# Issuing the small TensorE matmuls of the linear-attention stage one at a time between large ones

## The reference

```python
q = (x @ Wq.T).reshape(bsz, seq_len, H, HD).transpose(0, 2, 1, 3)
k = (x @ Wk.T).reshape(bsz, seq_len, KVH, HD).transpose(0, 2, 1, 3)
v = (x @ Wv.T).reshape(bsz, seq_len, KVH, HD).transpose(0, 2, 1, 3)
q = q * cos + _rotate_half(q) * sin
k = k * cos + _rotate_half(k) * sin
qf = jax.nn.elu(q) + 1.0
kf = jax.nn.elu(k) + 1.0
def step(carry, inp):
    state, z = carry
    q_s, k_s, v_s = inp
    state = state + k_s[..., :, None] * v_s[..., None, :]
    z = z + k_s
    num = jnp.einsum('bhe,bhed->bhd', q_s, state)
    den = jnp.einsum('bhe,bhe->bh', q_s, z)[..., None] + EPS
    return ((state, z), num / den)
```

## Time and profile before

| | |
|---|---|
| three runs | 2307.86, 2310.42, 2312.11 us (median 2310.42) |
| profiled execution | 2310.1 us from its first to its last instruction; its own whole time is listed nowhere else, and is taken as this span |
| first stage, fill (0 to 115 us) | TensorE waits for weights and inputs in part |
| first stage, steady (about 115 to 890 us) | 7 tiles of about 111 us |
| first stage, last tile and start of the second | about 890 to 962 us |
| rest | output projection, then the feed-forward, to 2310.1 us |
| busy over the span | TensorE 98%, weight loads 79%, VectorE 79%, ScalarE 55%, GpSimd 49% |

### The profile page before, as it was taken

One profiled execution on the slowest core, in us unless ns is written; L12 is line 12 of the kernel. 1 busy time (PEld: TensorE's weight loads), 2 busy tenths in 40 slices (PEclk: granted clock), 3 DMA queues, 4 the chain that ended last, 5 costly groups with the idle time before them and its releaser, 6 DMA issues.

```text
span 2310.1 us, 32819 instructions
## 1 busy us (share of the span) xinstructions
PE 2254.4 (98%) x10209; PEld 1823.0 (79%) x10209; DVE 1825.1 (79%) x2452; ACT 1273.1 (55%) x2285; POOL 1129.0 (49%) x1002
## 2 busy tenths in 40 slices
PE   7999999999999999999999989999999999999998
PEld 5778787787878786787777768888888888888887
DVE  7877777778686868787887896787888788878877
ACT  6666666666676767233334455454545554455443
POOL 4667676767676767455544733321242133303321
PEclk9999999999999999999999999999999999999999
DMA  4110101111120215777767541323233323222323
GB/s 153 37 65 37 68 34 66 47 58 62 39 73 28 73 60 192 255 246 254 245 229 261 187 140 62 123 78 113 79 101 92 118 81 98 92 82 83 98 67 101
DMA packets 132701, 252.75 MB, mean 109 GB/s; under 512 B 44576, under 2 KB 45344, under 8 KB 122880
## 3 DMA queue, kind: packets, MB, share of 16 engines
q1 hardware_dynamic: 132608, 251.60, 32.5%
HBM read 188.11 MB, written 63.44 MB: 109 GB/s over the span
## 4 chain that ended last, share of the span: by engine, by line
PE 71%; issue 11%; POOL 9%; DVE 5%; ACT 2%; DMA 1%; SPq 0%; POOLq 0%; ACTq 0%; DVEq 0%
PE pj L548 17%; PE pj L629 11%; PE pnum L629 6%; PE pj L643 5%; PE psc L629 5%; PE pj L558 4%; PE pst L629 4%; PE psc L643 4%; PE pnum L643 3%; PE psc L579 3%; PE pnum L597 3%; PE pnum L600 3%; PE pst L643 2%; POOL fa L1338 2%; PE pst L586 1%
## 5 line engine op out<-in xcount | busy, mean ns | idle before, releaser
L1368 POOL TENSOR_TENSOR wcs<-wcr 128x256 f32<-128x256 f32 x64 | 67.7, 1058 | 515.3 <-DVE wcl L1107 504.3
L1401 POOL TENSOR_TENSOR tb<-tb,sinb 128x512 f32<-128x512 f32 x160 | 224.0, 1400 | 91.7 <-ACT tb L928 90.9
L548 PE MATMUL pj<-xah,wqh 128*128 128x512 f32 x512 | 204.3, 399 | 4.3 <-DVE Kf L1243 3.0
L1404 POOL TENSOR_TENSOR Ql<-tb,Qh 128x512 fp32r<-128x512 f32 x128 | 169.7, 1328 | 70.2 <-ACT Qh L937 70.1
L478 PE MATMUL pj<-woh,oh 128*128 128x512 f32 x512 | 202.9, 396 | 0.0
L548 PE MATMUL pj<-xal,wqh 128*128 128x512 f32 x512 | 200.5, 392 | 0.0
L548 PE MATMUL pj<-xah,wql 128*128 128x512 f32 x512 | 200.5, 392 | 0.0
L478 PE MATMUL pj<-woh,ol 128*128 128x512 f32 x512 | 200.4, 391 | 0.0
L478 PE MATMUL pj<-wol,oh 128*128 128x512 f32 x512 | 200.3, 391 | 0.0
L1231 DVE TENSOR_TENSOR pj<-pj,cosb 128x512 f32<-128x512 f32 x160 | 111.1, 694 | 69.7 <-ACT tb L928 69.6
L629 PE MATMUL pj<-xch,wch 128*128 128x512 f32 x384 | 150.9, 393 | 7.9 <-DVE xcl L1113 4.7
(11 more groups left out here) (258 smaller groups left out, 7070.8 us busy)
## 6 DMA issues: line engine op xcount, KB each, us to landing
num_scratch<-no SPq DMA_DIRECT2D x128, 256.0 KB, 2.4
nt<-num_scratch SPq DMA_DIRECT2D x32, 1024.0 KB, 5.5
rb<-rden_scratch SPq DMA_DIRECT2D x32, 1024.0 KB, 6.3
wdr<-wd_scratch SPq DMA_DIRECT2D x128, 256.0 KB, 3.3
wcr<-in_wg SPq DMA_DIRECT2D x64, 256.0 KB, 2.8
wcr<-in_wu SPq DMA_DIRECT2D x64, 256.0 KB, 3.1
xst<-in_xT SPq DMA_DIRECT2D x34, 256.0 KB, 3.8
xr<-in_x SPq DMA_DIRECT2D x32, 256.0 KB, 5.6
```

The source lines that it names most:

```text
L548: last = nc.tensor.matmul(bank[:, :], w[:, b, :], x[:, b, :], start=(k == 0), stop=(k == 11))
L1401: nc.gpsimd.tensor_tensor(tb[c][:, :], tb[c][:, :], sinb[:, :], ALU.mult).then_inc(sin_done, 1)
L1404: nc.gpsimd.tensor_tensor(Ql[g % 2][:, c, :], (tb[c] if c else Kf)[:, :], f32(Qh[g % 2][:, c, :]), ALU.subtract).then_inc(lo_done, 1)
```

## The change

The 3 matmuls of a Z and the 4 transposes of a T are no longer issued where their event stands. The event only appends them to a list. The J, V, C and U events issue one from the head of the list after each of their large matmuls but the last (U's third matmul of the first half included); D issues none. The waits of a Z or a T are made directly ahead of its first small matmul, which is now inside another event. What is left in the list at the end of a tile's events is issued there. Each small matmul keeps its operands, its place among the small ones and its semaphore; the other engines' programs are as before.

```diff
+            def key_transpose(m, where, g, d, q):
+                if q == 0:
+                    bank_released(m, ("T", g, 0, d), where)
+                    pe.wait_ge(f_done, upto(m, d, NR, g * (G + 1)))
+                    if where == "start":
+                        pe.wait_ge(c_in, 16)
+                last = nc.tensor.transpose(pj[job_bank("T", g, 0)][:, q * CH:(q + 1) * CH], Kf[:, q * CH:(q + 1) * CH],
+                                           identb[:, :])
+                if q == NCH - 1:
+                    last.then_inc(t_done, 1)
+
+            def state_update(m, g, c, d, k):
+                u = g * NCH + c
+                hd = slice(g * HD, (g + 1) * HD)
+                if k == 0:
+                    pe.wait_ge(t_lo, upto(m, d, KV, g))
+                    pe.wait_ge(v_lo, upto(m, d, NCH, c))
+                    pe.wait_ge(s_lo, upto(m, d, NU, u))
+                a, b = ((Kth, Vh), (Kth, Vl), (Ktl, Vh))[k]
+                last = nc.tensor.matmul(pst[:, hd], a[:, c, :], b[:, c, hd], start=False, stop=(k == 2),
+                                        skip_group_check=True)
+                if k == 2:
+                    last.then_inc(state_done, 1)
...
+                short = []
+
+                def one_short():
+
+                    if short:
+                        kind, g, c, d, k = short.pop(0)
+                        if kind == "T":
+                            key_transpose(m, where, g, d, k)
+                        else:
+                            state_update(m, g, c, d, k)
+
                 for kind, g, c, d in events:
-                    if kind in "JVTD":
+                    if kind in "TZ":
+                        short += [(kind, g, c, d, k) for k in range(NCH if kind == "T" else 3)]
+                        continue
+                    if kind in "JVD":
...
                                 k += 1
+                                if k < 12:
+                                    one_short()
...
-                    elif kind == "T":
-                        pe.wait_ge(f_done, upto(m, d, NR, g * (G + 1)))
-                        if where == "start":
-                            pe.wait_ge(c_in, 16)
-                        for q in range(NCH):
-                            last = nc.tensor.transpose(bank[:, q * CH:(q + 1) * CH], Kf[:, q * CH:(q + 1) * CH], identb[:, :])
-                        last.then_inc(t_done, 1)
...
                             last = nc.tensor.matmul(out, a[:, 0, tok], b[:, 1:, tok], start=(k == 0), stop=(k == 2))
+                            if k < 2:
+                                one_short()
...
                             nc.tensor.matmul(num, a[:, c, hd], b[:, :, :], start=(k == 0), stop=False)
+                            one_short()
...
+                            if k < 2:
+                                one_short()
                         last.then_inc(unit_done, 1)
...
+                while short:
+                    one_short()
```

## The result

The changed kernel is slower: median 2331.2 us (2330.9 to 2333.0, 4 runs) against 2309.7 us of the kernel before in the same session (4 runs); ratio 1.009, 95% interval 1.0077 to 1.0103. The profiled execution is 2329.2 us long from first to last instruction, 19.1 us more than before. The forecast had the sign right and half of the size: 2320, range 2308 to 2328, and the measured time lies above that range.

The account below looks back on a forecast made before the run. TensorE was taken to set the pace of the first stage's seven steady tiles. The terms 3.9 + 2.4 - 0.3 + 0.7 + 3.0 = +9.7 us on the 2310.1 us span gave 2319.8, forecast as 2320, range 2308 to 2328.

Parts of the forecast that it names:

- The price of a small matmul: On TensorE a single small matmul costs 0.112 us as in a row, since weight loads run only one matmul ahead.
- The rival with loads further ahead: TensorE fetches weights further ahead, so small matmuls cost only their streaming time: -23 us, 2287 us; chance 0.10.
- The dearer exits: On TensorE, returning from small to large matmuls costs slightly extra, paid after each single one: +3.9 us over 8 tiles.
- Z22: Z22 moves behind U22's wait for `Al`, which had hidden it: +0.34 us in each of seven turns, +2.4 us.
- T3, C30 and J02: T3's transposes move behind C30's wait for `Ql`, -0.3 us; K3 comes late and J02 waits, +0.7 us.
- -0.3 us at C30: In three turns, two transposes behind C30's wait for `Ql` add 0.23 us each time, while 0.34 is absorbed.
- the slack of 0.7 us: Spare time, 0.70 us, before J02 starts at 583.99 and needs its bank; if it holds, late K3 costs J02 0.
- +0.7: J02 waits about 0.1 us per turn for its bank because K3 is late: +0.7 us.
- T2 ends about 1.1 us later: Later ends of T2, T0 and T1 cost nothing, as the next uses are 4 us or more behind.
- The last tile: A late fourth transpose delays K3 by 2.9 us, then VectorE's division and A30, which C32 awaits: +3.0 us.
- The rivals: Weights loaded further ahead, 2287 us (0.10); shifts mostly absorbed, about 2313 (0.25); keys late in every turn, 2328 (0.12).

Follow-up runs that it names:

- late rows: Changed kernel with each Z and T issued in a row again, at the place of its last single small matmul; 2331.3 us.
- singly in the loop only: Changed kernel with Z and T in rows in the unrolled tile before the loop and in the last tile, single only in the loop; 2322.5 us.

## Why the prediction was half right

- **The price of a small matmul.** Right: 0.114 us singly, 0.112 in a row, the large one behind it 0.45 us long, and the load one matmul ahead. The rival with loads further ahead is out by the changed kernel's own trace. The dearer exits, 3.9 us in the sum for eight tiles, were not far off: 2 to 3 us in seven turns, to which 3.4 of the 3.9 belong.
- **Z22.** Right in kind: the wait grew from 0.6 to 1.0 us in each of seven turns. But U22 itself starts 0.13 us earlier against D2, so only 0.23 us per turn stay, 1.6 us in all and not 2.4. For this move alone the times can't tell it from zero.
- **T3, C30 and J02.** The sum had -0.3 us at C30, taking its wait for `Ql` to occur in three turns only. The stretch around C30 costs +1.8. K3 does start over a microsecond late on ScalarE (a wait of 1.42 us in the turn at 477 us), but no wait of TensorE at J02 appears; the slack of 0.7 us held, so +0.7 was 0.
- **"T2 ends about 1.1 us later ... the next uses (Z20, J12, Z10) are 4 us or more behind, so I cost these at nothing."** This is the step that failed. I looked for who reads the result of the transposes and not for who waits to overwrite their input. VectorE's E30 writes `Kf` and waits for T2's end, and J32 waits for E30 with 0.08 us in hand. Seven times 0.80 us is 5.6 us, the largest single term of the loss; with T2 alone in a row 4.0 of them go.
- **The fill.** The prediction had no term for it. T1's lateness holds K1, the weight parts queue behind K1, and J21 waits 2.6 instead of 1.2 us and then runs at the lower clock: 3.8 us, of which the clock's 1.6 are in part luck.
- **The last tile.** Right in chain: C32 stands 2.7 us further behind C30, where 2.9 was forecast. The size is near: 3.0 forecast; 3.7 by the times and 3.2 by the table with T3 in a row, 4.0 for the whole tile. But J32's wait in this tile, which the forecast did not have, is in these 4.0, and so are the differences of the clock. So the size is in part luck.

So of the 20 us (19.2 by the spans and 0.9 for the late fill of the execution before), up to 3.0 (single issue), 1.6 (Z22) and 4.0 (last tile) were in the sum with their reason, 5.6 (J32), 1.8 (C30) and 3.8 (fill) were not. The large terms of the forecast came near; it missed by what it had at nothing, with the guard of `Kf` in front. Which part of C30's 1.8 us comes from Z22 and which from the transposes is open. The rivals were each about one place; none had the mechanism that decided.

## What to carry to other kernels

- When an instruction is moved later, list the semaphore that its end raises and find every wait on it in all engines' programs, those that guard a buffer against being overwritten included. A row that reads "costs nothing, the result is used much later" is only half of the question.
- Waits that are met by a few hundredths of a microsecond do not appear in a list of waits. They show as a record that is a little long (0.47 instead of 0.39 us). Even 0.27 us of waiting can hide behind the long record ahead, as at C30. The distance between starts tells.
- To separate the price of interleaving from that of lateness, issue the same work in a row at the late place, but do not judge by the total. Here the totals agreed within 0.1 us, while the starts of the same matmuls showed 2 us less for the issue and as much more for waits. Compare the places where nobody waits.

## What the runs showed of the hardware

- A matmul of 128 columns between two of 512 costs 0.114 us, twice its streaming time of about 0.055, because only one weight load runs ahead. Interleaving small with large ones gains nothing here; the three of Z10 cost 0.026 us more than in a row.
- TensorE fell to half its clock (granted 0.54 over the stretch) after a wait of 2.6 us in the fill: starts 0.427 instead of 0.227 us apart for about 3.5 us. In the late rows it kept its clock after a wait as long at the same place. Likewise the kernel before fell behind its wait of 2.0 us at 921.6 us (granted 0.52 from 922 to 925.5), and "singly in the loop only" kept 1.00 behind its wait of 2.0 us at 934.1. After waits of 0.9 us in the loop the changed kernel kept its clock in all seven turns.
